# Other tiles for the chain steps, two routing tiles in PSUM, and one GpSimd operation for the low part of hid

## The reference

```
x = x + 0.5 * ffn(layernorm(x))
x = x + mixer(layernorm(x))
x = x + 0.5 * ffn(layernorm(x))
```

## Time and profile before

| what | us |
|---|---|
| median of 3 runs | 712.45 |
| lowest, highest | 711.03, 712.47 |
| the profiled execution | 712.7 |
| its span, first to last instruction | 710.9 |

### The profile page before, as it was taken

How to read it: one execution, slowest core, us unless ns; L and a number is a source line. 1 busy time by engine, 2 the same in 40 slices (tenths; PEclk the granted TensorE clock), 3 DMA queues, 4 the chain that set the end, 5 groups by cost and what they waited for, 6 DMA issues and landing times. The chain is left out here.

```text
span 710.9 us, 10396 instructions
## 1 busy us (share of the span) xinstructions
PE 666.2 (94%) x3016; PEld 530.2 (75%) x3016; DVE 549.7 (77%) x1539; ACT 421.3 (59%) x801; POOL 483.5 (68%) x717
## 2 busy tenths in 40 slices
PE   5589999999999999899999999999989989898997
PEld 5468878777877888688876888688767768776785
DVE  5778778779869798788977798788968858756765
ACT  4445666575576656666566756666565556545553
POOL 1147568686777777776876867778776776775674
PEclk9899999999999999999999999999999999999999
DMA  7491909337191745719083462908338092460460
GB/s 189 107 209 43 229 4 191 80 92 165 35 207 30 164 92 114 157 27 212 18 191 79 110 133 66 201 5 190 67 75 166 4 192 62 103 138 16 108 148 16
DMA packets 60011, 78.84 MB, mean 111 GB/s; under 512 B 7697, under 2 KB 27185, under 8 KB 59953
## 3 DMA queue, kind: packets, MB, share of 16 engines
q1 hardware_dynamic: 59424, 77.91, 49.7%
q10 hardware_dynamic: 528, 0.26, 0.2%
HBM read 75.01 MB, written 3.15 MB: 110 GB/s over the span
## 5 line engine op out<-in xcount | busy, mean ns | idle before, releaser
L485 POOL TENSOR_TENSOR hid_lo<-hid,hid_hi 128x256 fp32r<-128x256 f32 x540 | 386.7, 739 | 187.3 <-ACT hid_hi L589 185.1
L728 DVE TENSOR_TENSOR weighted<-gate_ps,raw 128x512 f32<-128x512 f32 x256 | 175.0, 684 | 96.2 <-ACT gate_ps L581 85.4
L589 ACT ACTIVATE hid_hi<-hid 128x512 fp32r<-128x512 f32 x272 | 170.7, 628 | 113.7 <-DVE hid L741 111.7
L581 ACT ACTIVATE gate_ps<-gate_ps 128x512 f32<-128x512 f32 x256 | 148.6, 580 | 96.2 <-PE gate_ps L995 94.2
L741 DVE TENSOR_TENSOR hid<-weighted,up_ps 128x512 f32<-128x512 f32 x256 | 174.3, 681 | 7.3 <-DVE weighted L728 0.5
L1041 PE MATMUL down_ps<-hid_lo,wt_hi 128*128 128x512 f32 x272 | 108.5, 399 | 1.0 <-POOL hid_lo L485 0.8
L1038 PE MATMUL down_ps<-hid_hi,wt_hi 128*128 128x512 f32 x272 | 108.4, 399 | 0.0
L1039 PE MATMUL down_ps<-hid_hi,wt_lo 128*128 128x512 f32 x272 | 108.0, 397 | 0.0
L993 PE MATMUL gate_ps<-xT_hi,wt_hi 128*128 128x512 f32 x170 | 73.1, 430 | 6.4 <-DVE weighted L728 6.3
L993 PE MATMUL up_ps<-xT_hi,wt_hi 128*128 128x512 f32 x170 | 70.6, 415 | 7.2 <-DVE hid L741 7.2
L994 PE MATMUL gate_ps<-xT_lo,wt_hi 128*128 128x512 f32 x170 | 68.2, 401 | 0.0
(11 more groups left out here) (148 smaller groups left out, 1123.2 us busy)
## 6 DMA issues: line engine op xcount, KB each, us to landing
raw<-wT_hbm SPq DMA_DIRECT2D x64, 640.0 KB, 13.6
raw<-wT_hbm SPq DMA_DIRECT2D x32, 512.0 KB, 7.6
raw<-wT_hbm SPq DMA_DIRECT2D x32, 256.0 KB, 4.0
x_res<-in_L_attn_x SPq DMA_DIRECT2D x8, 256.0 KB, 3.3
x_ln<-in_L_attn_x SPq DMA_DIRECT2D x7, 256.0 KB, 3.4
out_x<-x SPq DMA_DIRECT2D x7, 256.0 KB, 2.3
raw<-in_L_ffn_gate_w SPq DMA_DIRECT2D x4, 256.0 KB, 5.7
raw<-in_L_ffn_up_w SPq DMA_DIRECT2D x4, 256.0 KB, 5.3
```

The source lines that it names most:

```text
L485: last = nc.gpsimd.tensor_tensor(hid_lo[s][:, cols], hid[s][:, cols], hid_hi[s][:, cols].bitcast(F32), ALU.subtract)
L581: nc.scalar.activation(bank[:, :] if j else silu_sb[:, :], bank[:, :], ACT.Silu).then_inc(silu_done, 1)
L589: nc.scalar.activation(hid_hi[s][:, :], hid[s][:, :], ACT.Copy).then_inc(hid_hi_done, 1)
L728: V.tensor_tensor(weighted[j % 2][:, :], gate_ps[n % BANKS][:, :], wb[:, j - 1, :], ALU.mult)\
```

## The change

Three things are changed.

1. The slots of most chain steps. The named tables are replaced: the middle units use `MIXER`, `ROUTE4`, `OUTPUT` and `NEXT` (k = 1) and `NORM4`, `PROJECT`, `ADD` and `PREPARE` (k = 4), and the first four and last five units have tables of their own. What each step does, its order within a slot and the waits are as before.
2. `gdiff` and `beats`, the differences of the group sums and their comparison (steps 14 and 15 of the routing), move from SBUF to columns 256 to 383 of the PSUM tile `routed`, where `logit_inv` was used earlier in the chain. Their operations are the same.
3. `hidden_low` is one operation of 512 columns in place of two of 256.

```diff
-        gdiff = sb("gdiff", [P, TT, NG * NG])
-        beats = sb("beats", [P, TT * NG, NG])
+        gdiff = routed[:, 256:320].rearrange("p (t x) -> p t x", t=TT)
+        beats = routed[:, 320:384].rearrange("p (x h) -> p x h", h=NG)
...
-        NEXT = {"stats 1": 12.5, "meanvar 1": 13, "norm 1": 14, "normalise 1": 15}
-        PREPARE = {"transpose 1": 0, "xT high 1": 0, "xT low 1": 0.5, "router 1": 2, "silu logits 1": 3,
-        ADD = {"copy ffn 1": 2, "transpose ffn 1": 4, "add ffn 1": 4}
-        PROJECT = {"stats 2": 1, "meanvar 2": 1.5, "norm 2": 2, "normalise 2": 3, "transpose 2": 9, "xT high 2": 9,
-                   "xT low 2": 9, "mixer gate": 11, "tanh gate": 11, "mixer value": 12, "copy value": 12,
-                   "add ln_b": 15}
-        MIXER = {"conv": (0, 0.5, 1, 2, 3, 4), "y high": 5, "y low": 5, "mixer out": 8, "mixer sum": 8,
-                 "stats 3": 14}
-        NORM4 = {"meanvar 3": 0, "norm 3": 0, "normalise 3": 1, "scale 3": 2, "x2": 10, "stats 4": 12,
-                 "meanvar 4": 13, "norm 4": 14, "normalise 4": 15}
-        ROUTE4 = {"router 4": 2, "silu logits 4": 3, "route 4": even(2, 12), "weights 4": 13}
+        ADD = {"copy ffn 1": 1, "transpose ffn 1": 4, "add ffn 1": 8.5}
+        PROJECT = {"stats 2": 1.5, "meanvar 2": 2, "norm 2": 2, "normalise 2": 3, "transpose 2": 9, "xT high 2": 9,
+                   "xT low 2": 9.5, "mixer gate": 10, "tanh gate": 10, "mixer value": 12, "copy value": 12,
+                   "add ln_b": 16}
+        NORM4 = {"meanvar 3": 0, "norm 3": 1, "normalise 3": 2, "scale 3": 3, "x2": 11, "stats 4": 11.5,
+                 "meanvar 4": 13, "norm 4": 14, "normalise 4": 16}
+        PREPARE = {"transpose 1": 0, "xT high 1": 1, "xT low 1": 1, "router 1": 2, "silu logits 1": 3,
+        MIXER = {"conv": (0, 0, 0, 0, 0.5, 1.5), "y high": 5, "y low": 5, "mixer out": 9, "mixer sum": 12.5,
+                 "stats 3": 13}
+        ROUTE4 = {"transpose 4": 0, "xT high 4": 0, "xT low 4": 0.5, "router 4": 3, "silu logits 4": 3,
+                  "route 4": even(2.5, 12.5), "weights 4": 13}
+        NEXT = {"stats 1": 13.5, "meanvar 1": 15, "norm 1": 14, "normalise 1": 16}
```

```diff
-                for half in range(2):
-                    cols = slice(half * SEQ, half * SEQ + SEQ)
-                    last = nc.gpsimd.tensor_tensor(hid_lo[s][:, cols], hid[s][:, cols],
-                                                   hid_hi[s][:, cols].bitcast(F32), ALU.subtract)
-                last.then_inc(hid_lo_done, 1)
+                nc.gpsimd.tensor_tensor(hid_lo[s][:, :], hid[s][:, :], hid_hi[s][:, :].bitcast(F32), ALU.subtract)\
+                  .then_inc(hid_lo_done, 1)
```

More of the change, by code:

```diff
@@ L317, in macaron_kernel @@
[L317 to L328, removed]
-        BEGIN = [at(FIRST, 1) + at(NEXT, 2),
-                 at(ADD, 0) + at(PROJECT_0, 0) + at(TAPS, 0) + at(PREPARE, 2) + at(NEXT, 3),
-                 at(MIXER_0, 0) + at(NORM4_0, 0) + at(ADD, 1) + at({**PROJECT, "stats 2": 4.5, "meanvar 2": 5,
-                                                                    "norm 2": 6, "normalise 2": 7}, 1)
-                 + at(PREPARE, 3),
-                 at(XT4, 0) + at(ROUTE4, 0) + at(MIXER, 1) + at(ADD, 2) + at({**NEXT, "stats 1": 11}, 4)]
@@ L336, in macaron_kernel @@
-        END = [at(MIXER_5, 5) + at(NORM4_5, 5) + at(XT4, 4) + at(ROUTE4, 4) + at(OUTPUT, 3)
-               + at({**PROJECT, "normalise 2": 9, "transpose 2": 11, "xT high 2": 11, "xT low 2": 11, "mixer gate": 14,
-                     "tanh gate": 14, "mixer value": 15, "copy value": 15}, 6),
-               at(MIXER_5, 6) + at(NORM4_5, 6) + at(XT4, 5) + at(ROUTE4, 5) + at(ADD, 7),
-               at(XT4, 6) + at(ROUTE4, 6) + at(OUTPUT, 4) + at(PROJECT, 7) + at(TAPS_7, 7),
-               at(REST_7, 7) + at(OUTPUT, 5),
-               at(OUTPUT, 6)]
+        ADD = {"copy ffn 1": 1, "transpose ffn 1": 4, "add ffn 1": 8.5}
@@ new lines, in macaron_kernel @@
+        END = [
+            [
+                ({"conv": (0, 0.5, 1, 2, 3, 4), "y high": 5, "y low": 5, "mixer out": 7, "mixer sum": 7.5,
[4 rows of a table added]
+                  "route 4": even(2.5, 12.5), "weights 4": 13}, 4),
+                ({"copy ffn 4": 2, "transpose ffn 4": 4, "halve ffn": 4, "add ffn 4": 7}, 3),
+                ({"stats 2": 0.5, "meanvar 2": 2.5, "norm 2": 2, "normalise 2": 8, "transpose 2": 10, "xT high 2": 10,
+                  "xT low 2": 11, "mixer gate": 11, "tanh gate": 13, "mixer value": 15, "copy value": 15,
+                  "add ln_b": 16}, 6),
+            ],
+            [
+                ({"conv": (0, 0, 0.5, 1.5, 2.5, 3.5), "y high": 4, "y low": 5, "mixer out": 7, "mixer sum": 8.5,
[4 rows of a table added]
+                  "route 4": even(2, 12), "weights 4": 12}, 5),
+                ({"copy ffn 1": 2, "transpose ffn 1": 5, "add ffn 1": 5}, 7),
+            ],
+            [
+                ({"transpose 4": 0, "xT high 4": 1, "xT low 4": 1.5, "router 4": 3, "silu logits 4": 3,
+                  "route 4": even(2.5, 12.5), "weights 4": 14}, 6),
+                ({"copy ffn 4": 2, "transpose ffn 4": 4, "halve ffn": 5, "add ffn 4": 8}, 4),
+                ({"stats 2": 0, "meanvar 2": 0, "norm 2": 0, "normalise 2": 2, "transpose 2": 9, "xT high 2": 9,
+                  "xT low 2": 8.5, "mixer gate": 10, "tanh gate": 11, "mixer value": 12, "copy value": 12,
+                  "add ln_b": 13}, 7),
+                ({"conv": (13, 13.5, 14, 14.5, 15, 15.5), "y high": 16, "y low": 16}, 7),
+            ],
+            [
+                ({"mixer out": 1, "mixer sum": 0.5, "stats 3": 0.5, "meanvar 3": 1, "norm 3": 1, "normalise 3": 2,
+                  "scale 3": 2, "x2": 3, "stats 4": 4, "meanvar 4": 4, "norm 4": 5, "normalise 4": 6,
+                  "transpose 4": 8, "xT high 4": 9, "xT low 4": 9, "router 4": 10, "silu logits 4": 11,
+                  "route 4": even(10, 14), "weights 4": 15}, 7),
+                ({"copy ffn 4": 3, "transpose ffn 4": 4, "halve ffn": 4, "add ffn 4": 4}, 5),
+            ],
+            [
+                ({"copy ffn 4": 1, "transpose ffn 4": 2, "halve ffn": 4, "add ffn 4": 8}, 6),
+            ],
+        ]
```

54 lines of the change are left out of this document (42 added, 12 removed), and 8 rows, old and new, of the table END.

## The result

The changed kernel took 685.18 us (median of 4 runs, 682.11 to 685.75), the kernel before 711.74 in the 4 runs beside it. The ratio is 0.963, with a 95% interval of 0.959 to 0.967. The forecast was 693.5, with a range of 685 to 707. A fifth execution on record, outside that median, took 688.24. The profiled execution is the shortest: 682.11 us, with a span of 680.3 us.

The account below looks back on a forecast made before the run. TensorE, busy 94% of the span, bounds the kernel, with about 38 us lost to holds and low clock. Unit terms summed to 22.8 us saved, less 3.5 for unseen waits, 19.3 off 712.7: 693.5 us, range 685 to 707.

Parts of the forecast that it names:

- rival B: Whole kernel: the holds go nearly all, the clock staying at its upper level; 30 us saved, 682.5; chance 0.06.
- Middle, k = 4: Four middle units: scale 3 behind norm 2 lets shift come sooner, shortening TensorE's three holds; 7.5 us saved.
- Middle, k = 1: Three middle units with the four taps together at slot 0: no hold now, can only lose; 1 us lost.
- rival C: Taps get no head start, hid of tile 0 is 1.1 us late: slower, 721 us; chance 0.10.
- hid_lo in one operation: GpSimd's low part of hid as one 512-column operation: nothing of its own, bounds 0 and 0.8 us saved.
- gdiff and beats: Routing tiles in PSUM: beats about 0.22 us, gdiff up to 1.5, nearly all beside slack; 0, 1.5 us either way.
- (1,7): Unit (1,7): xT high ahead of normalise 3 ends the 3.03 us hold; 0.9 left, 3.6 us saved.
- (4,4), (4,5): Two late units: holds and low clock shrink with normalise 4 sooner and the out product later; 4.7 and 2.8 us saved.
- (4,6) and (4,7): Last two units: (4,6) saves 3.7 us of holds and clock; (4,7) loses 0.65 to the copy, later weights cost 0.
- First units: Units (1,1) to (1,3): half of holds of 0.3 to 1.2 us taken as gone; 2.1 us saved.
- The allowance: Whole kernel: 3.5 us taken off the saving for waits that moved steps may make for each other.

Follow-up runs that it names:

- scale 3 late: Kernel before with one number changed: scale 3 of the middle k = 4 units at slot 3 instead of 2; 705.91 us, ratio 0.991.
- the tables alone: Changed kernel with gdiff and beats back in SBUF and hid's low part in two operations, so only the slots are changed; 687.31 us, ratio 0.965.

## Why the prediction was right, and where it was not

The time came out 8 us below the forecast, by the mechanisms that it named. It lies 0.2 us inside the range, and that it does is in part luck: of the four executions two (682.11 and 684.64) lie below the range. The profiled execution is rival B's case: the clock stayed at its upper level behind the first unit, and it took 682.11 us where B said 682.5.

- **Middle, k = 4: right, under-sized** (7.5 forecast, 11.4 measured). The chain shift, normalise, silu, weighted is shown by the move of scale 3 alone, which gives 1.25 of the 3.1 us of a unit. The hold of 0.35 us that I expected for the up product of tile 5 did not come. And I summed three holds, 2.2 us, where the second matmul behind each is stretched by about 0.1 us as well, and (4,1) had one more of 0.36 for weighted (at 288.05 us). The last 0.4 us of the 3.1 belong to the mark: silu now starts 0.3 us sooner behind the first gate product of a k = 1 unit. Marked by that product, the four k = 4 units save 10.8 us and the three k = 1 units 0.55.
- **Middle, k = 1: right** (-1.0 forecast, -0.4 measured, or 0.55 saved by the other mark, where I had said that they can only lose). The head start was 1.9 us against the 2 forecast, and is what rival C hung on. A hold for hid came in no k = 1 unit.
- **hid_lo in one operation: the term that failed.** I priced it by TensorE's idle time for hid_lo, 0 to 0.8 us. By itself it gave 5 to 6. Its own wait is worth 1.5 of that in the middle, by the starts of the matmuls; 2 more lie in (1,1), (4,4) and (4,6), since each low part ends 0.14 us sooner, and what queues behind it with it; the 1.5 of (4,5) are the clock's. Beside the new tables it costs 0.4 us in each k = 4 unit without the PSUM tiles.
- **gdiff and beats: sizes right, worth wrong.** beats came to 0.217 us and gdiff's longest to 1.359. "Nearly all beside slack" was true of the old tables (2 us alone). It is not of the new ones, where `add ffn 1` stands at slot 8.5 (4 before), right behind beats, and the transposes at 9 wait for it. There the tile's place is what lets the one operation be used: 40.05 against 39.43 us in (4,1) to (4,3).
- **(1,7): right** (3.6, 3.0). The 3.03 us hold is gone; of the 0.9 that I left, TensorE has 0.94 for xT low and 0.30 for tanh.
- **(4,4), (4,5): over-sized** (7.5 together, 4.5). The hold for w_tok in (4,4) stayed, 0.97 us. The clock's 1.7 us were part of the sum, and that step of the prediction does not hold: with one operation, and with scale 3 late, the hold at the end of (4,4) stood (1.86 and 2.21 us) and no low clock followed, 1.5 us in (4,5). So this term was not the hold's alone.
- **(4,6) and (4,7): 3.05 forecast, 3.6 measured, by luck.** Of its parts none was right, and the five other traces with these tables have 3.1 us at most. The unit's chain gained more than I had left to it. I missed the 2.09 us hold for the copy, which had stood at slot 3 of the table and behind normalise 3 and silu, and the later load, which I priced at 0 because a slot of slack covered the load's usual time. It does not cover a store that takes 1.4 to 2 us longer. The clock stayed up behind that hold in this trace; where it did not, (4,6) took 45.4 to 45.5 us and not 44.1.
- **First units**: 5.2 against 2.1. Halving the holds was a guess, and a low one.
- **The allowance** of 3.5 us for unseen waits was not needed: they were there (the copy, the load), and gains that I had not looked for were larger.

## What to carry to other kernels

Look in a strict queue for the long operation that nobody needs soon and that stands ahead of a small one on which others hang; here its place in the table was worth 5 us. When an operation of one engine is made longer, look at which operations of the engine that shares a port with it have two SBUF inputs, and at what stands behind those: here the merge paid by itself and cost time in the middle of the tuned order, until one input moved to PSUM. A load's slack should be counted against the longest time that its transfers show, not the median. And a unit's length from one trace holds the clock of that execution: a gain in a unit that the edit does not touch is a sign of it.

## What the runs showed of the hardware

- A 0.22 us operation of VectorE with both inputs in SBUF took up to 1.36 us beside GpSimd's operations of 1.29 us, and up to 0.75 (gdiff) and 1.12 (beats) beside two of 0.74. The output's place made no difference; one input in PSUM made it a steady 0.215 to 0.225.
- The same hold did or did not bring a stretch at the lower clock. At the start of (4,5) it was 2.22 us in the kernel before and 2.21 with scale 3 late, and the granted clock behind it 0.57 and 1.00. Behind the hold of 2.1 us for the copy in (4,6) it was 1.00 in the changed kernel and 0.54 with the tables alone; behind that of 3.03 us in (1,7), 1.00 in the kernel before and 0.66 with scale 3 late. Where it fell the unit was 1.3 to 1.5 us longer in the first two places.
- A 64 KB store to HBM landed in 1.5 to 1.6 us in most cases, and in 2.6 to 3.6 only where a 16 KB packet of an instruction fetch ran between its issue and its landing.
